# A two-layer convolution and linear-attention kernel: instruction slots set at four places, the image loaded ahead of the weights, and the pooled queries placed by ScalarE instead of VectorE

## The reference, cut to what matters

```python
x = x + conv3x3(_gn(x), weight)                 # layer 0, group norm over 32 groups first
# layer 1, on windows of 4 x 4 points (196 windows an image, 16 tokens each)
qkv = einsum('nchw,oc->nohw', windows(_gn(x)), qkv_w)     # 1x1 convolution
pooled = avg_pool5(qkv)                                   # 5x5 mean inside the window
q, k, v = relu(..), relu(..), ..                          # 64 heads of 8 channels, of qkv and of pooled
kv = k^T [v, 1];  out = q kv;  out = out[:-1] / (out[-1] + 1e-15)
x = x + batch_norm(proj_w out)
```

## Time and profile before

| | us |
|---|---|
| median of three runs | 2493.22 |
| the profiled execution | 2486.28 |
| its span | 2484.5 |
| TensorE busy in it | 2391.6 (96%) |
| VectorE busy | 1977.9 (80%) |
| ScalarE busy | 1282.2 (52%) |
| GpSimd busy | 1173.8 (47%) |

### The profile page before, as it was taken

The page is one execution under the profiler, slowest core; times in us unless marked ns, Lnnn a source line. Parts: engine busy times, 40 slices in busy tenths (PEclk is TensorE's granted clock), DMA queues, the critical chain, the costliest instruction groups (busy, mean ns, idle before and its releaser), DMA issues.

```text
span 2484.5 us, 112358 instructions
## 1 busy us (share of the span) xinstructions
PE 2391.6 (96%) x49576; PEld 2159.6 (87%) x49576; DVE 1977.9 (80%) x3608; ACT 1282.2 (52%) x3352; POOL 1173.8 (47%) x2364
## 2 busy tenths in 40 slices
PE   4999999999999999999999999999999999998998
PEld 4998889888898888988889888998889988897887
DVE  8888868888588886888868888688886888765885
ACT  2137751477414774167731677226771277613775
POOL 0027760377503774057730677206771167612776
PEclk9999999999999999999999999999999999999999
DMA  4000010000100002000010000100001000000000
GB/s 166 1 2 16 15 61 16 2 15 19 61 12 2 19 15 72 1 6 15 19 69 1 6 19 15 69 1 9 15 20 64 1 9 19 20 9 1 16 15 24
DMA packets 38962, 58.24 MB, mean 23 GB/s; under 512 B 4688, under 2 KB 36304, under 8 KB 36560
## 3 DMA queue, kind: packets, MB, share of 16 engines
q1 hardware_dynamic: 38736, 55.27, 6.3%
HBM read 29.57 MB, written 25.69 MB: 22 GB/s over the span
## 4 chain that ended last, share of the span: by engine, by line
PE 89%; DVE 5%; issue 3%; ACT 2%; DMA 0%; POOL 0%; SPq 0%; POOLq 0%; DVEq 0%
PE ps L337 31%; PE ps L408 15%; PE ps L356 10%; PE ps L397 9%; PE ps L363 8%; PE ps L383 8%; PE ps L372 4%; PE ps L417 3%; ACT ve L624 1%; DVE kvm L966 1%; DVE xh L926 1%; ACT kv_part L619 0%; DVE qs L977 0%; DVE kv_part L939 0%; PE ps L322 0%
## 5 line engine op out<-in xcount | busy, mean ns | idle before, releaser
L337 PE MATMUL ps<-dp,wc 128*128 128x392 f32 x4608 | 840.9, 341 | 7.6 <-ACT yb L658 5.6
L337 PEld LDWEIGHTS ps<-dp,wc 128*128 128x128 f32 x4608 | 815.3, 188 | 13.5 <-ACT yb L658 6.5
L1155 POOL TENSOR_TENSOR ve<-vpraw,vmask 128x1024 f32<-128x1024 f32 x200 | 392.7, 1964 | 390.1 <-ACT vpraw L635 390.1
L408 PEld LDWEIGHTS ps<-at,wp 128*128 128x128 f32 x3200 | 375.8, 192 | 51.3 <-DVE kvm L966 48.3
L926 DVE TENSOR_SCALAR xh<-xs,gn 128x128 f32<-128x128 f32 (+3 forms) x560 | 419.1, 800 | 1.6 <-PE ps L363 1.3
L408 PE MATMUL ps<-at,wp 128*128 128x128 f32 (+1 forms) x3200 | 405.7, 280 | 1.0 <-ACT yb L658 1.0
L1126 POOL TENSOR_TENSOR qm<-qraw 128x64 f32<-128x64 f32 x200 | 59.5, 298 | 726.2 <-ACT qraw L642 725.7
L606 ACT CAST dp<-dt 128x896 fp32r<-128x896 f32 x128 | 121.1, 946 | 470.9 <-PE ps L337 381.1
L356 PE MATMUL ps<-wkv,xt 128*128 128x512 f32 x1200 | 324.8, 406 | 1.6 <-issue 1.6
L624 ACT ACTIVATE ve<-ps,vmask 128x256 f32<-128x256 f32 x800 | 314.8, 491 | 0.0
L397 PEld LDWEIGHTS ps<-kvm,qs 64*32 64x32 f32 x25088 | 232.7, 105 | 81.0 <-issue 79.2
(11 more groups left out here) (87 smaller groups left out, 2902.1 us busy)
## 6 DMA issues: line engine op xcount, KB each, us to landing
out<-xs SPq DMA_DIRECT2D x224, 112.0 KB, 1.8
xs<-x SPq DMA_DIRECT2D x16, 1344.0 KB, 8.8
xs<-x SPq DMA_DIRECT2D x16, 224.0 KB, 2.7
xs<-w_conv SPq DMA_DIRECT2D x1, 2304.0 KB, 8.4
kvm<-w_kv SPq DMA_DIRECT2D x1, 512.0 KB, 14.4
wp<-w_proj SPq DMA_DIRECT2D x4, 128.0 KB, 8.0
wq<-w_q SPq DMA_DIRECT2D x1, 256.0 KB, 13.9
gav<-gavg SPq DMA_DIRECT2D x1, 64.0 KB, 8.1
```

Of the source, the lines that this page charges most:

```text
L337: last = nc.tensor.matmul(ps[:, conv_bank(v, mt), 0:CONV_N], wc[:, part_w, k, kt * TAPS + dy, mt * P:(mt + 1) * P], dp[:, kk % 2, part_d, ...
L408: last = nc.tensor.matmul(ps[:, BANK_A + mt, Y0:Y0 + n], wp[:, q, mt * P:(mt + 1) * P], at[:, q, e, 0:n], start=(q == 0), stop=(q == QUADS ...
L1155: nc.gpsimd.tensor_tensor(ve[:, t % 2, :, 1].rearrange("p e (n m) -> p e n m", m=DIM + 1)[:, :, :, 0:DIM], vpraw[:].rearrange("p (n m) -> ...
```

## The change

1. **Start.** Image 0 is loaded ahead of the convolution's weights, one DMA a half of the channels, and the weights come in two halves. GpSimd instead of VectorE combines the taps, half by half (six additions of 768 elements), and clears `ve`; ScalarE casts the high parts in eight pieces with the factor 0.5 in them; VectorE takes the low parts with the factor in the same instruction. VectorE begins with the statistics.
2. **Banks.** The product (chunk 1, third) writes banks 2 and 3 instead of 4 and 5, and the wait for the batch norm of the last tile (`y_ready`) moves from ahead of it to ahead of the first product of chunk 2.
3. **Slots.** `addr_align` stands at four places of every image: slot 152 as before, slot 92 ahead of the loop, slot 80 ahead of the first tile behind the loop and slot 56 ahead of the second. In the last image a fifth, slot 80, stands ahead of tile 0.
4. **Pooled queries.** ScalarE instead of VectorE places the pooled queries, as the first thing in its turn, ahead of `turned`.

```diff
+TAP_SCALE = (1.0, 0.5, 0.5, 1.0)
@@
+    if (c, kk) == (1, 2):
+        return BANK_O + mt
     return BANK_C[kk % 2][mt]
@@
-LEAD_SLOT = 152
+SLOT_LEAD, SLOT_FIRST, SLOT_LOOP, SLOT_OUT = 152, 80, 92, (80, 56)
@@
-        wouter = xp_flat[:, 0:TAPS_K].rearrange("p (a o) -> p a o", o=C)
+        wouter = qs[:].rearrange("p m e n -> p (m e n)")[:, 0:TAPS_K].rearrange("p (a o) -> p a o", o=C)
@@
-            sp.dma_start(wspace[:, 0:TAPS * TAPS_K], w_conv).then_inc(w_loaded, DMA)
+            for kt in range(KT):
+                sp.dma_start(xs[:, 0, kt, :], x[0, kt * P:(kt + 1) * P, :]).then_inc(x_first_loaded[kt], DMA)
+            sp.dma_start(wraw[:, 0:TAPS], w_conv[:, 0:1]).then_inc(w_loaded, DMA)
             sp.dma_start(gav[:], gavg).then_inc(gav_loaded, DMA)
-            load_x(0, 0)
-            load_x(0, 1)
+            sp.dma_start(wraw[:, TAPS:KT * TAPS], w_conv[:, 1:2]).then_inc(w_rest_loaded, DMA)
@@ TensorE
+            def at_slot(offset):
+                pe.addr_align(bass.FETCH_BLOCK_INSTRUCTIONS, offset=offset, max_nops=0)
@@ attention
                 if b + 1 < B:
                     pe.wait_ge(conv_added, 2 * v + 3)
+                else:
+                    at_slot(SLOT_FIRST)
                 for s in range(FIRST_LOOPED):
                     tile(t0 + s, s % 2, s, v)
+                at_slot(SLOT_LOOP)
                 with pe.Fori(0, LOOPED // 2) as i:
...
                 for s in range(FIRST_LOOPED + LOOPED, TILES):
+                    if s - FIRST_LOOPED - LOOPED < len(SLOT_OUT):
+                        at_slot(SLOT_OUT[s - FIRST_LOOPED - LOOPED])
                     tile(t0 + s, s % 2, s, v)
@@ later_chunks
                             last_tile(b - 1)
+                            continue
+                        if b >= 1 and (c, kk) == (2, 0):
                             pe.wait_ge(y_ready, b * TILES + 1)
-                            continue
@@ ScalarE
+            def taps_high(k, kt):
+                a = slice(kt * TAPS, (kt + 1) * TAPS)
+                nc.scalar.activation(wc[:, 0, k, a], wprod[k][:, a], ACT.Copy,
+                                     scale=TAP_SCALE[k]).then_inc(w_high, 1)
+            def pooled_q(b, t):
+                act.wait_ge(qsum_ready, b * TILES + t + 1)
+                if t >= 2:
+                    act.wait_ge(att_done, b * TILES + t - 1)
+                for a in range(2):
+                    last = nc.scalar.activation(
+                        qs[:, MT:G, t % 2, :].rearrange("p m (w a t) -> p m w a t", a=2, t=TOK)[:, :, :, a, :],
+                        qsum[:].rearrange("p (m w t) -> p m w t", m=MT, t=TOK),
+                        ACT.Relu, scale=qmaskp[:, a:a + 1])
+                last.then_inc(qp_ready, 1)
@@ attention
+                    if s + 1 < TILES:
+                        pooled_q(b, s + 1)
                     if s >= 0:
                         turned(b, s)
@@ VectorE
-            def pooled_q(b, t):
...
-            dve.wait_ge(w_loaded, DMA)
-            w_do(1, nc.vector.tensor_tensor(wouter, g0, g2, ALU.add))
...
+                nc.vector.scalar_tensor_tensor(wc[:, 1, k], wprod[k], TAP_SCALE[k], wc[:, 0, k].bitcast(F32),
+                                               ALU.mult, ALU.subtract).then_inc(w_ready, 1)
@@ GpSimd
+            def taps(kt):
+                a = slice(kt * TAPS, (kt + 1) * TAPS)
+                g0, gsum, g1, g2 = (w[:, a] for w in wprod)
+                pool.wait_ge(w_rest_loaded if kt else w_loaded, DMA)
+                nc.gpsimd.tensor_tensor(wouter[:, a], g0, g2, ALU.add).then_inc(w_step, 1)
...
+            nc.gpsimd.memset(ve[:], 0.0).then_inc(set_up, 1)
+            for kt in range(KT):
+                taps(kt)
```

More of the change, by code:

```diff
@@ L200, in build @@
         wsum = wspace[:, TAPS * TAPS_K:(TAPS + 1) * TAPS_K].rearrange("p (a o) -> p a o", o=C)
-        wouter = xp_flat[:, 0:TAPS_K].rearrange("p (a o) -> p a o", o=C)
+        wouter = qs[:].rearrange("p m e n -> p (m e n)")[:, 0:TAPS_K].rearrange("p (a o) -> p a o", o=C)
         wprod = (wraw[:, :, 0, :], wsum, wraw[:, :, 1, :], wraw[:, :, 2, :])
+        x_first_loaded = [sem(f"x_first_loaded{kt}") for kt in range(KT)]
         x_loaded = sem("x_loaded")
@@ L229, in build @@
         qraw_ready = sem("qraw_ready")
+        qp_ready = sem("qp_ready")
         at_ready = sem("at_ready")
@@ L717, in _ @@
             act.wait_ge(w_loaded, DMA)
-            for n, k in enumerate((0, 3, 1, 2)):
-                if n >= 2:
-                    act.wait_ge(w_step, n + 2)
-                nc.scalar.copy(wc[:, 0, k], wprod[k]).then_inc(w_high, 1)
+            taps_high(0, 0)
+            taps_high(3, 0)
+            act.wait_ge(w_step, 2)
+            taps_high(1, 0)
             root(0)
-            for v in range(2):
-                split(v)
+            act.wait_ge(w_step, 3)
+            taps_high(2, 0)
+            act.wait_ge(w_rest_loaded, DMA)
+            taps_high(0, 1)
+            taps_high(3, 1)
+            act.wait_ge(w_step, 5)
+            taps_high(1, 1)
+            split(0)
+            act.wait_ge(w_step, 6)
+            taps_high(2, 1)
+            split(1)
             act.wait_ge(c_loaded, CONSTS * DMA)
@@ L1169, in add_tile @@
                 last.then_inc(out_ready, 1)
+            def taps(kt):
[3 more added lines that the diff above has]
+                nc.gpsimd.tensor_tensor(wouter[:, a], g0, g2, ALU.add).then_inc(w_step, 1)
+                pool.wait_ge(w_step, 3 * kt + 1)
+                nc.gpsimd.tensor_tensor(gsum, wouter[:, a], g1, ALU.add).then_inc(w_step, 1)
+                pool.wait_ge(w_step, 3 * kt + 2)
+                nc.gpsimd.tensor_tensor(g1, wouter[:, a], g1, ALU.subtract).then_inc(w_step, 1)
+            nc.gpsimd.memset(ve[:], 0.0).then_inc(set_up, 1)
+            for kt in range(KT):
+                taps(kt)
             for b in range(B):
```

49 lines of the change are left out of this document (11 added, 38 removed).

## The result

| | before | after |
|---|---|---|
| median, us | 2493.2 | 2428.2 |
| lowest to highest, four runs | 2487.6 to 2496.8 | 2426.2 to 2429.1 |
| the profiled execution | 2486.28 | 2429.06 |
| its span | 2484.5 | 2427.2 |

The ratio is 0.974 (95% interval 0.9721 to 0.9759). The forecast was 2436, in a range of 2414 to 2474. By the profiled executions the gain is 57.2 us, where the sum of the terms said 57.5; by the medians it is 65. That the sum fits so well is partly luck: its terms are off by up to 7 us, in both directions.

A forecast was written before the change was run, and what follows sets the result against it. TensorE bounds the kernel with 89% of the chain, so only its standstills and the start pay. Terms 10 + 5.5 + 4 + 14 + 20 + 4 = 57.5 us off 2486.3 gave 2428.8 profiled, 2436 median; range 2414 to 2474.

The forecast's parts named there:

- The start: Image 0's start: first product at 25.9 us, second at 35.6 instead of 46.62; 10 us gained, between 7 and 12.
- From their end at 28.01 to the low part at 36.75 it is 8.74 us: At the start, from the statistics' end to VectorE's low part; carried over with one input exchanged, low part at 24.7.
- Banks and the stretch ahead of the tiles: Ahead of an image's tiles: no wait for the batch norm, 5.5 us; none for VectorE's placing of pooled queries, 4 us.
- The loop: Looped tiles: VectorE normalizes 0.52 us sooner without the placing, every tile takes 7.56 us; 14 us gained.
- ScalarE's price: ScalarE's two placing instructions, in a 0.76 us gap ahead of `at`, take 0.85 us, between 0.61 and 1.1.
- The ring: In the loop, pooled copies, GpSimd's spreading and sum, ScalarE's placing, `at`, again: 7.44 us a tile, 0.1 to spare.
- The ring rival: The cycle of ScalarE and GpSimd sets the loop's period: only 43.5 to 20 us saved, 2450 to 2473; chance 0.24.
- Behind the loop: Tiles 21 and 22: aligned slots cut code stalls from 28.8 to 8 us; 20 us gained, between 10 and 28.8.
- At the loop's entry: Ahead of and in the loop: slot 92 removes the second of the 7.6 us of stalls; 4 gained, between 0 and 7.6.
- the rival at 2541: Three new alignment jumps an image lose the code prefetch, with a second stall behind each: 48 us slower; chance 0.07.
- what the prediction named as a sign of being wrong: Code alignment: stalls standing right behind the three new jumps would show the prediction wrong; no size given.
- From the profiled execution to the median: Whole kernel: the median lies 6.9 us above the profiled execution, and the gain carries over, 2428.8 becoming 2436.

The follow-up runs named there:

- The placing alone: The kernel before with only part 4, ScalarE instead of VectorE placing the pooled queries: 2473.8 us, ratio 0.9948.
- the shortened spreading: The kernel before with GpSimd's spreading of the pooled values cut from 1024 elements to 64: 2474.5 us, ratio 0.9923.
- The slots alone: The kernel before with only part 3, the alignments at four places: 2454.3 us, ratio 0.9867.
- moving the jump: The changed kernel with the alignment ahead of the loop moved up inside tile 0, ahead of its transposes, at slot 44: 2420.6 us.

## Why the prediction was right, and where it was not

- **The start**, 10 forecast, 6.6 measured at the second product. The step that failed is "From their end at 28.01 to the low part at 36.75 it is 8.74 us", carried over to a stretch that now has GpSimd's additions beside it. It took 13.6 us from the end of the statistics at 15.52. Four small instructions of VectorE wait out the additions, by 1.06, 1.49, 0.23 and 1.52 us, 4.3 together. That GpSimd's additions would run at that time was in the forecast; that they would hold VectorE was not, although show a normalization of 2.63 us beside a spreading. The additions themselves took 1.81 us each instead of 1.5.
- **Banks and the stretch ahead of the tiles**, 9.5 forecast, 10.0 measured. Near in both: 0.99 us an image for the banks where the wait was 0.8, and about 0.5 an image for the placing where 4 us in all were said; 1.3 us of the waits for VectorE's addition stayed.
- **The loop**, 14 forecast, 15.3 measured. The late step (normalization, then values, low part, mask) was named rightly, and so was the turn in which it is late: all 56 tiles that got shorter follow a turn with four normalizations, and these start 0.52 us sooner and are as long as before. The placing alone gives the same. What the forecast did not name is why four normalizations are so long in the first place: 1.6 of their 2.63 us are spent behind GpSimd's spreading, as the shortened spreading shows.
- **ScalarE's price.** The pair took 0.91 us against 0.85, and was covered. The ring has 0.3 us of room, where 0.1 was forecast. The ring rival was the most likely of the rivals and did not happen.
- **Behind the loop**, 20 forecast, 27.2 measured. The idle time was sized well: the stalls of tiles 21 and 22 went from 25.8 us (the other 3.0 of the 28.8 stand in the first two looped tiles of the last image) to 5.3, so 20.5 us, and the next block was asked for 1.1 us ahead of tile 21 in seven images, where 1.0 was taken. The term was mis-sized because the stalls' cost in before was counted as their idle time alone, where in four images the clock fell too, 1.5 to 1.8 us each; that is nearly all of the other 6.7 us.
- **At the loop's entry**, 4 forecast, 1.6 lost. "Slot 92 puts the boundaries 164 and 420 instructions into the first tile ... so that the second stall goes" held in six of eight images (0.4 us is left in two), but the first got worse by more than the 40 instructions that it comes sooner: with the jump right ahead of the loop and the placing moved, the next block came late in all eight images. The slots alone gained 4.8 us here, and the placing alone lost 10.4: what failed is that the placing was given no price at the loop's entry. "Gain between 0 and 7.6" had no end below nothing.
- **The jumps** lost no prefetch in general: the rival at 2541 was wrong by a wide margin. Between the starts of tiles 3 and 20 TensorE's code queue shows no fetch at all, in any image. The one loss is at the entry, where a stall of 0.8 to 1.4 us does stand in the tile behind the new jump, in part what the prediction named as a sign of being wrong; moving the jump mended it.
- **From the profiled execution to the median** 6.9 us were carried over unchanged. They were no constant: after the change the median lies 0.8 us below the profiled execution. That put the median 7.8 us below the forecast. By the relation of time and clock over 29 runs the 6.9 us were most likely falls of the clock, which went with the stalls; it is not shown for these four runs.

## What to carry to other kernels

Look at what another engine does beside an instruction before taking its duration into a sum: VectorE's 0.16 us became 1.7 beside a GpSimd addition, and its two normalizations 0.60 or 2.18, with nothing in the waits to show it. Where TensorE stands still for more than a microsecond now and then, read the granted clock behind the gap, and take the spread of the runs as a part of the cost; stalls that went took most of the spread with them here (14.4 us over 29 runs before, 2.8 over four after). Put a jump for code alignment ahead of slow instructions, not right ahead of the dense ones that it is meant to help.

## What the runs showed of the hardware

- Four of VectorE's instructions of two elements from SBUF to SBUF (TENSOR_TENSOR and TENSOR_SCALAR) ended with GpSimd's running addition at the start of the changed kernel, and a TENSOR_SCALAR of two elements took 2.32 us beside a GpSimd memset, ending at 4.69 where that ended at 4.67. A RECIPROCAL at 21.38, in the middle of an addition, took 0.17, and a TENSOR_SCALAR of 840 elements was not held either (1.00 us).
- In before, two stalls of 1.4 to 2.1 us some ten us apart behind the loop were followed in some images by a granted clock of 0.72 to 0.88 over six us, in others not, with the same instructions.
- A hardware loop whose pass is 927 instructions (912 of TensorE, 15 of its instruction stream's own), over three and a half blocks of 256, is passed ten times an image with no stall for code from tile 3 on, and TensorE's code queue shows no fetch between the starts of tiles 3 and 20.
- At this loop's first entry the stall for code follows from when the block behind the loop's head is asked for: 2.4 to 4.3 us ahead of the loop no stall, 0.8 ahead to 0.6 behind 0.4 to 1.6 us, in 104 of 104 images of thirteen kernels.
